# Layer 0: one tile of each of 15 groups copied row by row by SyncE and ScalarE through DRAM; layer 2's boundary with ScalarE's high parts first

## The reference, cut to what matters

```python
# layer 0
e = edge_attr @ We + be
msg = relu(x[src] + e)                      # one row of x per edge
aggr = segment_sum(msg, dst)
h = gelu((x + aggr) @ W1 + b1) @ W2 + b2
# layer 1: four graph attention passes (a, b, c, d)
# layer 2: five steps of
h_all = einsum('nd,ted->nte', h, W) + b     # 4 edge types
a = segment_sum(h_all[src, etypes], dst)
h = gru_cell(a, h)
# layer 3: 16 relation types
agg = relu(segment_sum((h @ W[rel])[src] * norm, dst))
```

## Time and profile before

| | us |
|---|---|
| median of 3 runs (lowest, highest) | 8204.98 (8196.1, 8208.67) |
| the profiled execution | 8197.95 |
| its span, first to last instruction | 8196.7 |

### The profile page before, as it was taken

One profiled execution on the slowest core, in us unless ns is written; L12 is line 12 of the kernel. 1 busy time (PEld: TensorE's weight loads), 2 busy tenths in 40 slices (PEclk: granted clock), 3 DMA queues, 4 the chain that ended last, 5 costly groups with the idle time before them and its releaser, 6 DMA issues.

```text
span 8196.7 us, 138876 instructions
## 1 busy us (share of the span) xinstructions
PE 5763.4 (70%) x50188; PEld 5280.0 (64%) x50188; DVE 4654.4 (57%) x8857; ACT 2315.4 (28%) x6265; POOL 5284.6 (64%) x5497
## 2 busy tenths in 40 slices
PE   5888635887466666488876999979679999823333
PEld 3666535886366665377764888976669999723232
DVE  7777535776488887398884777763122222333333
ACT  0000023443134443044442666651011111112221
POOL 7777777777777776777777777777730000077776
PEclk9999767998588887599996999996889999966666
DMA  5554123332255552133323777753568988611111
GB/s 186 180 172 132 30 70 76 80 80 56 82 145 147 145 146 80 49 90 91 87 68 109 219 218 219 218 149 118 192 251 327 354 326 326 263 27 28 28 27 27
DMA packets 432169, 1151.54 MB, mean 140 GB/s; under 512 B 151749, under 2 KB 225350, under 8 KB 394168
## 3 DMA queue, kind: packets, MB, share of 16 engines
q0 software_dynamic: 225888, 471.27, 22.7%
q1 hardware_dynamic: 205596, 671.39, 22.6%
HBM read 1018.78 MB, written 120.93 MB: 139 GB/s over the span
## 4 chain that ended last, share of the span: by engine, by line
PE 35%; POOL 28%; issue 16%; DVE 12%; DMA 5%; ACT 2%; DVEq 1%; ACTq 0%; SPq 0%; POOLq 0%
POOL pool L1579 15%; PE ps L1543 11%; PE ps L2259 10%; POOL ACC L521 5%; POOL cnt_d L899 5%; PE ps L540 3%; PE ps L1224 3%; DVE ACC L496 2%; DMA pool<-d_h,srcT_s 2%; PE ps L1829 2%; POOL pool L521 2%; DVE pool L1432 2%; ACT ACC L1496 2%; DVE pool L1380 1%; POOL edge_d L1336 1%
## 5 line engine op out<-in xcount | busy, mean ns | idle before, releaser
L1543 PE MATMUL ps<-pool 128*106 128x128 f32 (+2 forms) x19344 | 2400.5, 283 | 50.9 <-DVE pool L1432 50.9
L1543 PEld LDWEIGHTS ps<-pool 128*106 128x106 f32 (+2 forms) x19344 | 2292.0, 170 | 61.2 <-DVE pool L1432 60.8
L1496 ACT ACTIVATE ACC<-ps 72x256 f32 (+1 forms) x2418 | 1010.4, 418 | 1485.2 <-PE ps L1543 1293.7
L521 POOL DMA_INDIRECT ACC<-t,ACC x410 | 386.9, 944 | 1245.7 <-DVE ps L2093 1121.0
L899 POOL DMA_INDIRECT cnt_d<-pool x806 | 842.8, 1046 | 317.3 <-issue 240.5
L1432 DVE TENSOR_TENSOR pool<-pool,ps 128x1024 f32<-128x1024 f32 (+1 forms) x807 | 927.4, 1209 | 0.0
L1579 POOL DMA_INDIRECT pool<-d_h,srcT_s x806 | 764.3, 948 | 245.5 <-issue 179.4
L1579 POOL DMA_INDIRECT pool<-b_h,srcT_s x806 | 764.2, 948 | 245.5 <-issue 231.2
L496 DVE TENSOR_TENSOR ACC<-ACC,ps 65x128 f32 (+1 forms) x1612 | 454.4, 282 | 809.9 <-PE ps L540 581.9
L1579 POOL DMA_INDIRECT pool<-a_h,srcT_s x738 | 708.1, 960 | 224.8 <-issue 215.9
L2259 PE MATMUL ps<-pool,ACC 128*128 128x192 bf16 x8600 | 767.8, 249 | 76.4 <-DMA ACC<-cnt_d 76.4
(11 more groups left out here) (346 smaller groups left out, 8856.2 us busy)
## 6 DMA issues: line engine op xcount, KB each, us to landing
ACC<-cnt_d SPq DMA_DIRECT2D x172, 1600.0 KB, 8.7
pool<-cnt_d SPq DMA_DIRECT2D x88, 1600.0 KB
cnt_d<-pool SPq DMA_DIRECT2D x26, 3200.0 KB
ACC<-t SPq DMA_DIRECT2D x1536, 0.2 KB
ACC<-key_d SPq DMA_DIRECT2D x17, 1280.0 KB
ACC<-key_d SPq DMA_DIRECT2D x21, 768.0 KB
ACC<-key_d SPq DMA_DIRECT2D x26, 512.0 KB
ACC<-key_d SPq DMA_DIRECT2D x13, 1024.0 KB
```

Of the source, the lines that this page charges most:

```text
L521: g.indirect_dma_start(out=gb[b][:, k, :], out_offset=None, in_=table, in_offset=bass.IndirectOffsetOnAxis(ap=idx[:, c:c + 1], axis=0)).th ...
L1496: a.activation(win[:, 0:NPL, bass.ds(reg, 128)], pl[0].rearrange("p (i c) -> p i c", c=128), ACT.Copy).then_inc(*(tile_out if last else A) ...
L1543: mm = t.matmul(o, gbr[:, tile % RT, M * i:M * i + M], oh, start=True, stop=True)
```

## The change

In layer 0, the first tile (k = 0) of 15 groups isn't gathered by GpSimd. SyncE does it for the 9 groups of `SP_L0` (17, 22, 27, 33, 38, 43, 49, 54, 59), ScalarE for the 6 of `ACT_L0` (20, 28, 36, 44, 52, 60). From iteration 7 on, SyncE issues 24 row copies of 256 bytes in each of its iterations, x to a DRAM strip, with node numbers loaded into registers 8 at a time; ScalarE issues 16 in each of its own, with one load of 16 numbers. When 128 rows have landed, one copy of the strip puts the tile into its buffer, 4 or 5 groups before its use. SyncE's row copies stand at the end of its iteration, behind the edge load, the key row, the fill and the segments.

In layer 2, ScalarE's order for rows 8 to 24 changes from high(b), mid(b), high(b+1) to high(b+1), mid(b). The gate's parts keep nearly their places.

```diff
+ROWS_FROM, SP_ROWS, ACT_ROWS = 7, 24, 16
+SP_L0 = [u for u in (ROWS_FROM - (-128 * (i + 1) // SP_ROWS) + 4 for i in range(NG)) if u < NG]
+ACT_L0 = [u for u in (ROWS_FROM + 128 * (i + 1) // ACT_ROWS + 5 for i in range(NG)) if u < NG]
+L0_STAGED = SP_L0 + ACT_L0
...
-                for k in range(tiles(gi)):
+                for k in range(first(gi), tiles(gi)):
...
+        def first_gathered(gi):
+            return 1 if gi in L0_STAGED else 0
...
+        staged_l0 = dram("l0_staged", (len(L0_STAGED), 128, 64))
...
+        def sync_rows_l0(gi):
+
+            for e0 in range(SP_ROWS * (gi - ROWS_FROM), SP_ROWS * (gi - ROWS_FROM + 1), 8):
+                i, p0 = e0 // 128, e0 % 128
+                if e0 >= 0 and i < len(SP_L0):
+                    if p0 == 0:
+                        s.wait_ge(sp_nos_in[i % 2].sem, 16 * (i // 2 + 1))
+                    _, regs = nc.values_load_multi_w_load_instructions(
+                        sp_nos[i % 2][0:1, p0:p0 + 8], engines=[mybir.EngineType.SP], min_val=0, max_val=NP - 1,
+                        skip_runtime_bounds_check_because="sources are node numbers")
+                    for e in range(8):
+                        s.dma_start(staged_l0[i, p0 + e:p0 + e + 1, :],
+                                    I["x"][bass.ds(regs[e], 1), :]).then_inc(*sp_staged[i % 2].one())
+                    if p0 == 120:
+                        sync_numbers_l0(i + 2)
+
+        def sync_tile_l0(u):
+
+            i = SP_L0.index(u)
+            s.wait_ge(sp_staged[i % 2].sem, 16 * 128 * (i // 2 + 1))
+            s.wait_ge(eam.sem, 2 * (u - GB0) + 1)
+            s.dma_start(gb0[u % GB0][:, 0, :], staged_l0[i]).then_inc(*sp_put.one())
...
@@ scalar_l0, at the end of group gi
+                if gi + 5 in ACT_L0:
+                    scalar_tile_l0(gi + 5)
+                scalar_rows_l0(gi)
...
@@ tensor_l0, before L783
+                if gi in SP_L0:
+                    t.wait_ge(sp_put.sem, 16 * (SP_L0.index(gi) + 1))
+                if gi in ACT_L0:
+                    t.wait_ge(act_put.sem, 16 * (ACT_L0.index(gi) + 1))
...
@@ sync_l0, at the end of group gi
+                if gi + 4 in SP_L0:
+                    sync_tile_l0(gi + 4)
+                sync_rows_l0(gi)
...
@@ scalar_step
-            scalar_rows(r0, AHEAD, AHEAD + 3)
-            if stp:
-                scalar_gate_rz(stp - 1, NCOL - 1)
-            scalar_rows(r0, AHEAD + 3, AHEAD + 4)
-            if stp:
-                scalar_gate_n(stp - 1, NCOL - 1)
-            scalar_rows(r0, AHEAD + 4, AHEAD + 5)
-            if stp:
-                scalar_state(stp - 1, NCOL - 1)
-            scalar_rows(r0, AHEAD + 5, NB)
+            scalar_row_high(r0, AHEAD)
+            for b in range(AHEAD, NB):
+                if stp and b == AHEAD + 2:
+                    scalar_gate_rz(stp - 1, NCOL - 1)
+                if b + 1 < NB:
+                    scalar_row_high(r0, b + 1)
+                scalar_row_mid(r0, b)
+                if stp and b == AHEAD + 2:
+                    scalar_gate_n(stp - 1, NCOL - 1)
+                if stp and b == AHEAD + 4:
+                    scalar_state(stp - 1, NCOL - 1)
```

More of the change, by code:

```diff
@@ L506, in gpsimd_tile_flags, with gpsimd_gather @@
                     in_=tile_flag[:, j, :], in_offset=None).then_inc(*flagged.one())
-        def gpsimd_gather(table, idx, gb, arrived, read, parts, free=0, ready=None, tiles=lambda gi: K):
+        def gpsimd_gather(table, idx, gb, arrived, read, parts, free=0, ready=None, tiles=lambda gi: K, first=lambda gi: 0):
             nb = len(gb)
@@ L515, in gpsimd_gather @@
                     gpsimd_tile_flags()
-                for k in range(tiles(gi)):
+                for k in range(first(gi), tiles(gi)):
                     c = gi * K + k
-                    part = [i for i, (k0, m) in enumerate(parts) if k0 == k]
+                    part = [i for i, (k0, m) in enumerate(parts) if max(k0, first(gi)) == k]
                     if part and gi >= nb:
@@ L659, in gathered_tiles @@
             return K - PG if gi >= FIRST else K
+        def first_gathered(gi):
+            return 1 if gi in L0_STAGED else 0
         def arrivals_l0(gi):
-            return 16 * sum(gathered_tiles(x) for x in range(gi % GB0, gi + 1, GB0))
+            return 16 * sum(gathered_tiles(x) - first_gathered(x) for x in range(gi % GB0, gi + 1, GB0))
+        staged_l0 = dram("l0_staged", (len(L0_STAGED), 128, 64))
+        sp_nos, act_nos = ([ns[0:1, 256 * q + 128 * j:256 * q + 128 * j + 128].bitcast(I32) for j in range(2)] for q in range(2))
@@ new lines, in build, with sync_numbers_l0, scalar_numbers_l0 @@
+        sp_nos_in, act_nos_in = ([dsig(f"l0_{q}_numbers{j}_in") for j in range(2)] for q in ("sp", "act"))
+        sp_staged, act_staged = ([dsig(f"l0_{q}_staged{j}") for j in range(2)] for q in ("sp", "act"))
+        sp_put, act_put = dsig("l0_sp_tile_put"), dsig("l0_act_tile_put")
+        def sync_numbers_l0(i):
+            if i < len(SP_L0):
+                s.dma_start(sp_nos[i % 2], I["srcR0"][i:i + 1, :]).then_inc(*sp_nos_in[i % 2].one())
+        def scalar_numbers_l0(i):
+            if i < len(ACT_L0):
+                a.dma_start(act_nos[i % 2], I["srcR0"][len(SP_L0) + i:len(SP_L0) + i + 1, :]).then_inc(*act_nos_in[i % 2].one())
@@ new lines, in sync_tile_l0, with scalar_rows_l0 @@
+        def sync_tile_l0(u):
[3 more added lines that the diff above has]
+            s.dma_start(gb0[u % GB0][:, 0, :], staged_l0[i]).then_inc(*sp_put.one())
+        def scalar_rows_l0(gi):
+            e0 = ACT_ROWS * (gi - ROWS_FROM)
+            i, p0 = e0 // 128, e0 % 128
+            if e0 >= 0 and i < len(ACT_L0):
+                if p0 == 0:
+                    a.wait_ge(act_nos_in[i % 2].sem, 16 * (i // 2 + 1))
+                _, regs = nc.values_load_multi_w_load_instructions(
+                    act_nos[i % 2][0:1, p0:p0 + ACT_ROWS], engines=[mybir.EngineType.Activation], min_val=0, max_val=NP - 1,
+                    skip_runtime_bounds_check_because="sources are node numbers")
+                for e in range(ACT_ROWS):
+                    a.dma_start(staged_l0[len(SP_L0) + i, p0 + e:p0 + e + 1, :],
+                                I["x"][bass.ds(regs[e], 1), :]).then_inc(*act_staged[i % 2].one())
+                if p0 + ACT_ROWS == 128:
+                    scalar_numbers_l0(i + 2)
@@ L664, in by_products, with scalar_tile_l0 @@
+        def scalar_tile_l0(u):
+            i = ACT_L0.index(u)
+            a.wait_ge(act_staged[i % 2].sem, 16 * 128 * (i // 2 + 1))
+            a.wait_ge(eam.sem, 2 * (u - GB0) + 1)
+            a.dma_start(gb0[u % GB0][:, 0, :], staged_l0[len(SP_L0) + i]).then_inc(*act_put.one())
         def by_products(u):
@@ L759, in scalar_l0 @@
             a.wait_ge(*mark["l0_ready"])
+            scalar_numbers_l0(0)
+            scalar_numbers_l0(1)
             for gi in range(NG):
@@ L801, in sync_l0 @@
             s.wait_ge(*zeroed.now())
+            sync_numbers_l0(0)
+            sync_numbers_l0(1)
             for gi in range(NG):
@@ L813, in gpsimd_l0 @@
             gpsimd_gather(I["x"], srcT, gb0, arrived_l0, eam, PARTS, EARLY_GB, mark["l0_ready"],
-                          gathered_tiles)
+                          gathered_tiles, first_gathered)
         sync_w0()
@@ L2536 @@
         arr[name] = pad(a[x], NT * 128).reshape(NT, 128)[[K * gi + K - 1 for gi in ROW_GROUPS]].reshape(1, 128 * NROW)
+    arr["srcR0"] = pad(a["src"], NT * 128).reshape(NT, 128)[[K * gi for gi in L0_STAGED]]
     arr["ewT"] = lay_t(a["edge_weight1"][:, 0])
```

## The result

| | before | after |
|---|---|---|
| median (lowest, highest), us | 8205.95 (8196.1, 8208.67) | 8609.03 (8603.95, 8614.28) |
| ratio, with its 95% interval | | 1.0499 [1.0483, 1.0514] |
| span of the profiled execution | 8196.7 | 8612.9 |
| L783 of group 61 starts | 912.32 | 1347.97 |
| layer 2, from the start of its first high part to the start of layer 3's first row list | 1435.8 | 1414.7 |

The span grew by 416.2 us. Layer 0 lost 1347.97 - 912.32 = 435.6 and layer 2 gave 21.1 back, which leaves 1.7 for everything else. The forecast was 8211, with +20 and -14.

The account below looks back on a forecast made before the run. Layer 0 was bound by GpSimd's gathers, then by SyncE's list; layer 2's boundary by a ScalarE and VectorE chain. +20 - 14 = +6 on 8196.7, with the runs' median 7 above the profiled execution, gave 8211; range 8164 to 8262.

Parts of the forecast that it names:

- +20 and -14: Layer 0 20 us longer with SyncE as its bound; layer 2's four boundaries 14 us shorter, bounds 8 and 24.
- (b): Layer 0, SyncE's 1152 row copies at .42 us and 144 loads make it the bound, layer 0 +20 us.
- the sum: SyncE's whole list over iterations 7 to 54 of layer 0: 699 us, 14.6 an iteration, against GpSimd's 13.7.
- the 484 of the forecast: Layer 0, SyncE's 1152 row copies at .42 us each: 484 us.
- Rival 3: Layer 0, SyncE held longer by fills (2 to 3.5 us each) or dearer loads: 8250 to 8290, chance .18.
- The load of 8: Layer 0, SyncE's register load of 8 numbers: .85 us, outer bounds .27 and 1.23; 144 loads, 127 us.
- TensorE waits for the first: Layer 0, edge loads queue behind SyncE's row copies and TensorE waits for them; group 55 28 us late.
- my 12.8: Layer 0, the consumers' us a group when rows are there; the last six groups give 8 us back.
- (c): Layer 0, ScalarE's 16 rows and one load, 7.7 us an iteration, hide in SyncE's 14.6: 0, upper bound 43.
- (f): Layer 2's boundary, four times: TensorE's own order becomes the limit, 3.5 us each, 14 us, bounds 8 and 24.
- Rival 4: Layer 2's part does nothing (clock dip, DMA): 14 us less gain in every case; no chance of its own.
- 1.276 a gather: Layer 0, GpSimd's time per gather; fifteen gathers leave it, 19.1 us, all on the layer's bound.

Follow-up runs that it names:

- 61 of 64 floats: Changed kernel, strip in DRAM, each row copy of SyncE and ScalarE moving 244 bytes instead of 256: 8692.83 us, ratio 1.0602.
- half fills: Strip in SBUF, 16 rows by SyncE and 16 by ScalarE an iteration, each 3200 KB fill cut in two: 8157.65 us, ratio 0.9941 to before.
- 16 and 16: Changed kernel with the strip in SBUF and 16 rows an iteration by SyncE instead of 24, 16 by ScalarE: 8158.41 us, ratio 0.9949 to before.
- constant source: Changed kernel, strip in DRAM, SyncE's row copies taking their source row from a constant address instead of a register: 8503.25 us, ratio 1.0361 to before.

## Why the prediction was wrong

1. **Failed: the row copy's price in (b).** "There the target is SBUF; a one-row store to DRAM takes .236 to issue against .225, so I take .42." That store reads SBUF. The copy in the change reads DRAM and writes DRAM, and no row of before had that pair. It measured .781 a row, +415 us of the 429 by which the sum was short. The experiments take it apart: with the strip in SBUF the 1152 rows cost 577 us instead of 899, so 322 go with the pair of places; with the fills away as well they cost 490, so 87 go with the fills; and 490 is, within 6, the 484 of the forecast. The text kept outer bounds of .27 and 1.23 for the load of 8 but gave the row, eight times as many instructions, none at all; at 11.5 us for each .01 it was the term that could move the result most. The store that it took as its neighbour was, besides, a single one, of 15.9 KB.
2. **Rival 3 came true beside it, near its size.** In the changed kernel the rows issued within 14 us of a fill took 66 us more than their median asks, 3 us for each of 22 fills, where I had 2 to 3.5; with the strip in SBUF taking the fills away gave rows 87 us back, 4 a fill. The other 46 us by which rows of the changed kernel were slow lie away from the fills, and what holds them no run shows. The argument against (a row copy carries only 256 bytes) was wrong: small copies are held. The segment load indeed hardly is (.59 in the strip-in-SBUF kernel, .44 without fills). What put the time at 8609 and not at the 8250 to 8290 of this rival is point 1.
3. **The load of 8** took .526 in the median (.685 mean), not .85, 23 us less than forecast. My value between two lines through other loads was wrong. The Trainium skill ("DMA: Bandwidth & Descriptors", Latency and other measured facts) gives a floor of about 600 ns for a tensor load; .526 for eight numbers lies below it, as .268 for one did. In the kernels with the strip in SBUF the same load took .78, and 1.06 with 61 of 64 floats; why, no run here shows.
4. **Right: SyncE becomes the bound, through the edge loads.** "TensorE waits for the first": 47 waits, 446 us. Group 55 started 7.6 us after its edge load's issue (forecast 6). The last six groups took 11.15 each, not 12.8, so they gave back 18 instead of 8; my 12.8 from groups 5 to 17 was not the fastest that the consumers can go.
5. **ScalarE at 0 (c)** was wrong alone and hidden together. Its row is .78 and not .42, near the .84 at which I wrote 43 us late; and its load of 16 took 2.17 on average, not 1.02. Alone it cost 44.7 us at group 61. That this is close to my 43 is luck, since the two prices differ from mine and the bound beside it was GpSimd and not SyncE. Beside SyncE's 23.5 us it costs next to nothing, as the text said of SyncE's 14.6; that it hides there is owed to point 1.
6. **Layer 2 (f)**: the mechanism right, the size 3.5 a boundary, measured 21.1/4 = 5.3, inside its bounds of 2.4 and 5.6. The half-pace rows vanished with TensorE's idle time, the clock going from 0.90 to 1.00, so this term goes near its upper bound. From the places of the text's 34.5 us to the merge it is now 28.9 (7016.72 to 7045.64), the figure worked out for no dip, though its terms (25.7 + 3) add up to 28.7. Rival 4 didn't come.
7. **GpSimd's 1.276 a gather** held roughly where nothing else limited: six tiles gave 9.6 us at group 61 (7.7 by the row), twelve 19.1 and, with half fills, 13.3 (15.3 by the row). These are single executions, and group 61 of before and of layer 2's part alone, where layer 0 is the same, are 2.2 apart.

What stays open: why a copy from DRAM to DRAM costs SyncE twice the issue. Neither the cut in 16 nor the register address explains it; whether a source in SBUF with a target in DRAM would go at .236 in a burst wasn't tried. Nor was 16 and 16 rows through DRAM. An estimate from the list of after: 16 x .781 + 2 x .72 + 2.3 for the old duties + .3 = 16.5 us an iteration, over the 13.3 an iteration of the kernel with 16 and 16 in SBUF, so by this estimate it would lose.

## What to carry to other kernels

Price an issue by its two places, DRAM or SBUF, from a row that has the same pair, and give the term with the most instructions the widest bounds. Before work is put on an idle engine, add up that engine's whole iteration against the pace of the bound: the same idea with 16 rows for SyncE and a strip in SBUF takes 27 us off the kernel with layer 2's part (8158 against 8185), with 24 rows through DRAM it adds 424. The fills of 3200 KB here held up the small copies issued after them, on both hardware queues, so leave room for such fills in the sum.

## What the runs showed of the hardware

- Issue of a 256-byte row copy on a hardware queue, medians: DRAM to SBUF .228 us (SyncE), .213 (ScalarE); DRAM to DRAM .492 and .500 to .534, .591 with a constant source, and .556 for 244 bytes uncut. Two register instructions and gaps add .18 (SyncE) or .16 (ScalarE).
- DRAM-to-DRAM rows in a burst leave at one in .63 (constant source) to .68 us (register source), and .75 with 244 bytes.
- After a fill of 3200 KB, copies of 256 bytes were slow to issue for 10 to 14 us (strip in SBUF: means of .87 to 1.06 at 3 to 10 us, .29 at 10 to 14, .23 later; after 1600 KB .50 at 3 to 6 and .24 at 6 to 10); the longest in layer 0 was 4.5 us (16 and 16, SBUF) and 6.5 (constant source, DRAM), and without fills none of SyncE's took over .343. ScalarE's rows were held too (mean .60 at 6 to 10 us after a fill against .22 later, strip in SBUF), though the fills stand on SyncE's queue.
- Register loads, medians: 8 numbers .526, 16 numbers 1.2 (ScalarE). In the strip-in-SBUF kernels 8 took .78 to .84, with 61 of 64 floats 1.06.
